# A decoder on one core: the attentions over the 77 context rows with softmax on the query side

## What is computed

```python
Q = proj_split(q, w_q)      # (B, 16, 512, 8)
K = proj_split(k, w_k)      # (B, 16, 77, 8)
V = proj_split(v, w_v)
scores = jnp.einsum('bhqd,bhkd->bhqk', Q, K) / jnp.sqrt(jnp.float32(DK))
scores = jnp.where(mask == 0, jnp.float32(-1000000000.0), scores)
attn = jax.nn.softmax(scores, axis=-1)
ctx = jnp.einsum('bhqk,bhkd->bhqd', attn, V)
ctx = ctx.transpose(0, 2, 1, 3).reshape(q.shape[0], -1, D)
return jnp.einsum('bsd,ed->bse', ctx, w_o)
```

## Time and profile before

| | us |
|---|---|
| median of 3 runs (2273.33 to 2279.63) | 2277.38 |
| the profiled execution's own time | 2252.73 |
| its span, first to last instruction | 2250.9 |
| mean granted TensorE clock in it | 0.899 |

### The profile page before, as it was taken

One profiled execution on the slowest core, in us unless ns is written; L12 is line 12 of the kernel. 1 busy time (PEld: TensorE's weight loads), 2 busy tenths in 40 slices (PEclk: granted clock), 3 DMA queues, 4 the chain that ended last, 5 costly groups with the idle time before them and its releaser, 6 DMA issues. The chain is left out here.

```text
span 2250.9 us, 34926 instructions
## 1 busy us (share of the span) xinstructions
PE 1797.8 (80%) x12404; PEld 1094.5 (49%) x12521; DVE 1477.1 (66%) x3404; ACT 1048.0 (47%) x2229; POOL 393.3 (17%) x575
## 2 busy tenths in 40 slices
PE   5768967999965999995779999993489889687872
PEld 3445542343334566663556666662245444344661
DVE  4436757888846555555546677686879999566524
ACT  2325534777721333332526555551167777365221
POOL 0110021000023444443110000001200000100374
PEclk8879977999975999998879999996589999799896
DMA  3000000000015588884000000000000000000373
GB/s 86 0 1 1 1 1 0 1 1 1 1 54 212 211 301 300 297 298 146 1 1 1 1 1 1 1 1 17 0 1 2 1 1 2 1 1 1 110 216 115
DMA packets 42797, 134.65 MB, mean 60 GB/s; under 512 B 7117, under 2 KB 22529, under 8 KB 37443
## 3 DMA queue, kind: packets, MB, share of 16 engines
q1 hardware_dynamic: 36587, 121.17, 15.5%
q0 software_dynamic: 4992, 10.23, 1.5%
q10 hardware_dynamic: 1048, 1.01, 0.2%
HBM read 123.29 MB, written 11.45 MB: 60 GB/s over the span
## 5 line engine op out<-in xcount | busy, mean ns | idle before, releaser
L153 POOL TENSOR_SCALAR rstd<-MV 128x2 f32<-128x2 f32 (+1 forms) x100 | 24.4, 244 | 1109.2 <-DVE MV L125 1102.6
L845 DVE TENSOR_REDUCE l1aM<-PS 128x2 f32<-128x1024 f32 x128 | 152.8, 1220 | 22.9 <-PE PS L601 20.8
L763 ACT ACTIVATE l1aE<-PS 128x512 f32<-128x512 f32 x256 | 140.9, 595 | 49.0 <-PE PS L630 45.6
L1575 PE MATMUL PS<-WB,H 128*128 128x512 f32 x312 | 142.6, 600 | 1.2 <-ACT H L1692 1.2
L763 ACT ACTIVATE l3aE<-PS 128x512 f32<-128x512 f32 (+3 forms) x256 | 102.5, 443 | 47.6 <-PE PS L634 44.9
L2463 DVE TENSOR_REDUCE M<-PS 128x1 f32<-128x589 f32 x128 | 92.5, 764 | 36.0 <-PE PS L2274 36.0
L845 DVE TENSOR_REDUCE l3aM<-PS 128x2 f32<-128x256 f32 (+3 forms) x128 | 101.3, 819 | 20.6 <-PE PS L603 19.6
L2372 ACT COPY PT<-PS 128x512 f32<-128x512 f32 x128 | 69.1, 590 | 92.9 <-PE PS L2285 92.6
L2378 ACT ACTIVATE E<-PS,M 128x589 f32<-128x589 f32 x128 | 95.8, 761 | 22.7 <-DVE M L2463 22.6
L1692 ACT ACTIVATE H<-PS,WB 128x128 f32<-128x128 f32 x156 | 44.5, 368 | 121.3 <-PE PS L1566 121.3
L873 DVE SCALAR_TENSOR_TENSOR l3aE<-l3aE,l3aLB 128x2048 f32<-128x2048 f32 (+1 forms) x64 | 94.9, 1483 | 2.7 <-ACT l3aE L763 2.7
(11 more groups left out here) (695 smaller groups left out, 4666.6 us busy)
## 6 DMA issues: line engine op xcount, KB each, us to landing
WB<-in_experts SPq DMA_DIRECT2D x39, 1798.0 KB
TB<-mixed_tails SPq DMA_DIRECT2D x39, 384.0 KB
WB<-in_experts SPq DMA_DIRECT2D x39, 384.0 KB, 4.2
WB<-mixed_out SPq DMA_DIRECT2D x8, 256.0 KB, 4.8
YB<-expert_out SPq DMA_DIRECT2D x8, 256.0 KB, 4.7
WB<-in_fold SPq DMA_DIRECT2D x1, 1676.0 KB, 7.0
cols_l2x_sb<-in_cols_l2x SPq DMA_DIRECT2D x1, 1154.0 KB, 10.2
mixed_tails<-in_tails SPq DMA_DIRECT2D x1, 1152.0 KB, 8.7
```

Source lines behind the costliest of these rows:

```text
L763: nc.scalar.activation(E[0:kn, home(m, kt) + j, q0:S], PS[0:kn, 4 + n % 2, q0:S], ACT.Exp, scale=SCALE).then_inc(exp_done, 1)
L845: v.tensor_reduce(M[:, m % 2, qt, 2 * hp:2 * hp + 2], PS[:, bank:bank + 2, 0:kc], AX, ALU.max, negate=True).then_inc(pair_free, 1)
L1575: mm(o, H1[:, i % 3, c * P:(c + 1) * P], mid_w(i, c), start=(c == 0), stop=False)
```

## The change

`cross_attention` takes the place of `attention16` for l0x and l3x. Q, K and V are projected once a batch (K and V for all four batches at once) and stay fp32, with the biases added. KS holds K eight times, each copy with only one head's rows of a 64-row half left (`own`), so that a product of 64 rows with four of these copies gives four heads' scores. The unit of work is S: one tile of 128 queries and eight heads, 128 x 1232 scores in two banks, made by four fp32 products, one in each 64x64 quadrant of the array, of 308 columns each (in l0x behind two bf16 mask products). There are two units to a query tile, 32 to a stage. VectorE takes the maximum over the 77 keys of each head and subtracts it into E; ScalarE takes the exponential of all 1232 in place. X turns E head by head (eight fp32 transposes into two banks, each emptied by a ScalarE copy into ET), and O multiplies, for a query tile, each of the 16 heads' turned probabilities (77 x 128, the stationary operand) with its 8 columns of V and a column of ones; VectorE divides. C, W, Y, N go by half batches, for which the norm's helpers are cut in two. `CROSS` is the order: for tile i, X of unit 2i+2, S of unit 2i+4, O of tile i, X of 2i+3, S of 2i+5, with Q, C, W, Y, N placed between by hand. GpSimd makes KS for batches 1 to 3. The three-part splits, gathers, the second scores and the turned maxima are gone in these stages. `setup` no longer loads or makes `maskT`.

```diff
+CROSS = (
+    (("X", 1, 0, 0), ("X", 1, 0, 1), ("S", 2, 0), ("O", 0), ("X", 1, 1, 0), ("X", 1, 1, 1), ("S", 2, 1)),
+    {0: ((0, ("Q", 1)), (5, ("Y", -1, 0)), (6, ("C", -1, 1))), 1: ((3, ("N", -1, 0)),),
+     2: ((0, ("W", -1, 1)), (4, ("C", 0, 0)), (5, ("Y", -1, 1))), 3: ((0, ("W", 0, 0)), (4, ("N", -1, 1)))},
+)
+def cross_attention(k, name, w, mask=None):
...
+                if kind == "K":
+                    mm(PS[:, 5, 0:BT * SC], w["wk"], k.CT[:, :, :].rearrange("p b n -> p (b n)"), start=True, stop=True).then_inc(kb_ready, 1)
...
+                elif kind == "S":
+                    n = u[1]
...
+                    if n >= 2:
+                        pe.wait_ge(shifted, n - 1)
+                    for g in range(2):
+                        if mask is not None:
+                            mm(PS[:, 2 * (n % 2) + g, 0:CW], k.ident_b, mask[:, qt:qt + 1, :].broadcast_to([P, HG, SC]), start=True, stop=False,
+                               skip_group_check=True)
+                    for half in range(2):
+                        for g in range(2):
+                            c0, rows = qt * P + 64 * half, slice(64 * g, 64 * g + 64)
+                            ins = mm(PS[64 * half:64 * half + 64, 2 * (n % 2) + g, 0:CW], Q[rows, b % 2, c0:c0 + 64],
+                                     KS[rows, b, HG * p:HG * p + HG, :].rearrange("p j n -> p (j n)"), start=mask is None, stop=True,
+                                     skip_group_check=True)
+                    ins.then_inc(s_ready, 1)
+                elif kind == "X":
+                    n, g = u[1:]
+                    if g == 0:
+                        pe.wait_ge(exped, n + 1)
+                    if n:
+                        pe.wait_ge(et_taken, 2 * n + g - 1)
...
+                    for j in range(HG):
+                        ins = nc.tensor.transpose(PS[0:SC, 4 + g, j * P:(j + 1) * P], E[:, n % 2, g, j, :], k.ident)
+                    ins.then_inc(e_turned, 1)
+                elif kind == "O":
...
+                    pe.wait_ge(et_taken, 4 * i + 4)
...
+                    for p in range(2):
+                        for g in range(2):
+                            for j in range(HG):
+                                h = HG * (p + 2 * g) + j
+                                ins = mm(PS[:, 6, h * DA:(h + 1) * DA], ET[:, (2 * i + p) % 4, HG * g + j, :], Va[:, b, h, :], start=True, stop=True)
+                    ins.then_inc(o_ready, 1)
...
+                elif kind == "S":
+                    n = u[1]
+                    act.wait_ge(shifted, n + 1)
+                    e = E[:, n % 2].rearrange("p g j n -> p (g j n)")
+                    nc.scalar.activation(e, e, ACT.Exp, scale=SCALE).then_inc(exped, 1)
+                elif kind == "X":
+                    n, g = u[1:]
+                    act.wait_ge(e_turned, 2 * n + g + 1)
...
+                    nc.scalar.copy(ET[:, n % 4, HG * g:HG * g + HG, :].rearrange("p j q -> p (j q)"), PS[0:SC, 4 + g, :]).then_inc(et_taken, 1)
...
+                elif kind == "S":
...
+                    dve.wait_ge(s_ready, n + 1)
+                    sc = PS[:, 2 * s:2 * s + 2, 0:CW].rearrange("p g (j n) -> p g j n", n=SC)
+                    v.tensor_reduce(top[:, s], sc, AX, ALU.max, negate=True).then_inc(maxed, 1)
+                    dve.wait_ge(maxed, n + 1)
+                    if n >= 2:
+                        dve.wait_ge(e_turned, 2 * n - 2)
+                    v.tensor_tensor(E[:, s], sc, top[:, s].unsqueeze(3).broadcast_to([P, 2, HG, SC]), ALU.add).then_inc(shifted, 1)
+                elif kind == "O":
+                    i = u[1]
+                    dve.wait_ge(o_ready, i + 1)
+                    o = PS[:, 6, 0:H * DA].rearrange("p (h d) -> p h d", d=DA)
+                    step(v.reciprocal(rec[:, :], o[:, :, DK]))
+                    step.wait()
...
@@
-                act.dma_start(maskT_i[:, :], dram["maskT"]).then_inc(mask_landed, 16)
@@
-                for m, o in ((mask_i, mask_b), (maskT_i, maskT_b)):
-                    step(v.tensor_scalar(o[:], m[:], 0, -1.0, ALU.not_equal, ALU.add))
-                    step.wait()
-                    step(v.tensor_scalar(o[:], o[:], -NEG, None, ALU.mult))
+                step(v.tensor_scalar(mask_b[:], mask_i[:], 0, -1.0, ALU.not_equal, ALU.add))
+                step.wait()
+                step(v.tensor_scalar(mask_b[:], mask_b[:], -NEG, None, ALU.mult))
@@
-            attention16(k, "l0x", W["l0x"], k.CT, (mask_b[:, :, :], maskT_b[:, :]))
+            cross_attention(k, "l0x", W["l0x"], mask_b[:, :, :])
@@
-            attention16(k, "l3x", W["l3x"], k.CT)
+            cross_attention(k, "l3x", W["l3x"])
```

More of the change, by code:

```diff
@@ L113, in norm_stats, with norm_half_stats, norm_half_apply @@
     def norm_stats(self, dve, y, step, b):
+        for h in HALVES:
+            self.norm_half_stats(None if y is None else y[:, h], step, b, h)
+    def norm_half_stats(self, y, step, b, h):
         v = self.nc.vector
[L116 to L119, removed]
-                step.wait()
-            for t in range(h.start, h.stop):
-                step(v.bn_stats(self.S6[:, b, t, :], self.R[:, b, t, :]))
-            step.wait()
-            for t in range(h.start, h.stop):
-                ins = v.bn_aggr(self.MV[:, b, t, :], self.S6[:, b, t, :])
-            ins.then_inc(self.statted, 1)
+        if y is not None:
+            step(v.tensor_tensor(self.R[:, b, h], y, self.X[:, b * NT + h.start:b * NT + h.stop, :], ALU.add))
+            step.wait()
+        for t in range(h.start, h.stop):
+            step(v.bn_stats(self.S6[:, b, t, :], self.R[:, b, t, :]))
+        step.wait()
+        for t in range(h.start, h.stop):
+            ins = v.bn_aggr(self.MV[:, b, t, :], self.S6[:, b, t, :])
+        ins.then_inc(self.statted, 1)
     def norm_apply(self, dve, normed, b, n):
+        for i in range(len(HALVES)):
+            self.norm_half_apply(dve, normed, b, n, i)
+    def norm_half_apply(self, dve, normed, b, n, i):
         v = self.nc.vector
[L131 to L137, removed]
+        h = HALVES[i]
+        dve.wait_ge(self.statted, 2 * n + i + 1)
+        dve.wait_ge(self.rooted, 2 * (2 * n + i) + 2)
+        for t in range(h.start, h.stop):
+            v.tensor_scalar(self.X[:, b * NT + t, :], self.R[:, b, t, :], self.MV[:, b, t, 0:1], self.rstd[:, b, t:t + 1],
+                            ALU.subtract, ALU.mult).then_inc(normed, 1)
     def norm_vector(self, dve, y, step, normed, b, n):
@@ L3044, in decoder_kernel @@
         mask_b = k.sb("mask_b", [P, NT, SC], BF16)
-        maskT_b = k.sb("maskT_b", [SC, S], BF16)
         kmask_u = k.sb("kmask_u", [1, BT, SC], U8)
@@ L3077, in setup @@
             mask_i = k.sb("mask_i", [P, NT, SC], I32)
-            maskT_i = k.sb("maskT_i", [SC, S], I32)
             causal = k.sb("causal", [P, 2, P])
@@ L3139, in _ @@
                     step(v.tensor_copy(o, const[i]))
-                dve.wait_ge(mask_landed, 48)
+                dve.wait_ge(mask_landed, 32)
                 step(v.tensor_copy(k.causal_b, causal[:, 0, :]))
                 step(v.tensor_copy(k.causalT_b, causal[:, 1, :]))
-                for m, o in ((mask_i, mask_b), (maskT_i, maskT_b)):
-                    step(v.tensor_scalar(o[:], m[:], 0, -1.0, ALU.not_equal, ALU.add))
-                    step.wait()
-                    step(v.tensor_scalar(o[:], o[:], -NEG, None, ALU.mult))
+                step(v.tensor_scalar(mask_b[:], mask_i[:], 0, -1.0, ALU.not_equal, ALU.add))
+                step.wait()
+                step(v.tensor_scalar(mask_b[:], mask_b[:], -NEG, None, ALU.mult))
                 for b in (1, 3):
@@ L3283, in packs @@
     biases.update(l0a_ball=np.concatenate([a["L0_attn_b_v"], a["L0_attn_b_shell"], a["L0_attn_b_charge"]]), l0a_bo=a["L0_attn_b_out"])
-    cols["l0x"] = attn16_pack(*(a["L0_xattn_w_" + n].T for n in "qkvo"))
+    i = np.arange(P)[:, None]
+    own8 = (i // 32 % 2 == np.arange(2 * HG) // HG) & (i // DK % HG == np.arange(2 * HG) % HG)
+    cols["l0x"] = dict(attn16_pack(*(a["L0_xattn_w_" + n].T for n in "qkvo")), own=own8)
     cols["l0f"] = dict(wr=a["L0_ffn_W_r"].T, wk=a["L0_ffn_W_k"].T, wv=a["L0_ffn_W_v"].T,
@@ L3311, in packs @@
     f = "L3_xattn_"
-    cols["l3x"] = attn16_pack(*(a[f + "W" + n] for n in "qkvo"), a[f + "bq"], a[f + "bk"])
+    cols["l3x"] = dict(attn16_pack(*(a[f + "W" + n] for n in "qkvo"), a[f + "bq"], a[f + "bk"]), own=own8)
     biases.update(l3x_bv=a[f + "bv"], l3x_bo=a[f + "bo"])
@@ L3373, in lay_out @@
               "causal": np.stack([later, later.T], 1).astype(np.float32), "decay": decay.astype(np.float32), "terms": stack_terms(),
-              "mask": mask.reshape(NT, P, SC).transpose(1, 0, 2), "maskT": mask.T,
+              "mask": mask.reshape(NT, P, SC).transpose(1, 0, 2),
               "kmask": kmask.reshape(B, 1, SC), "experts3": experts3.reshape(8 * P, 6 * P)}
```

159 lines of the change are left out of this document (added).

## The result

The changed kernel takes 2330.4 us (median of 4 runs, 2308.3 to 2334.8) beside 2276.3 us for the kernel before (4 runs, 2273.3 to 2279.6): a ratio of 1.0218, 95% interval 1.015 to 1.0286. The forecast was 2332.0.

The account below looks back on a forecast made before the run. No engine bounds the whole kernel, but both stages are mostly bound by TensorE. Terms of 5.4 + 8.3 + 26 + 13 + 2 give 54.7 us slower: 2307.5 us profiled, 2332 as a median; range 2282 to 2365.

Parts of the forecast that it names:

- The bound: Both stages, l0x and l3x: mostly bound by TensorE, busy 123 of 145 and 112 of 142 us before the change.
- VectorE and ScalarE: Per tile in both stages, priced for 1232 scores a unit: VectorE 7.2 us, ScalarE 4.8 and 0.5 us.
- TensorE at 2.4 GHz: TensorE's work a tile at full clock: 7.7 us in l3x, 8.3 in l0x, of which O 3.5 us.
- The hand-over and the score unit: VectorE and TensorE waiting for each other make tiles 8.2 us (l3x) and 8.55 (l0x); a score unit takes 0.95 us.
- the walk: Tile order followed, 15.5 tiles plus head and tail: l3x 147.3 us (+5.4), l0x 152.8 us (+8.3).
- The clock: Falls to 1.2 GHz behind O, 1.75 us each: one a tile in l3x (26 us), one in two in l0x (13).
- The sum: Both stages together: 5.4 + 8.3 + 26 + 13 + 2 = 54.7 us slower, 2332 us as a median.
- carried-over 24.6 us: Whole kernel: the earlier runs' median, 2277.38 us, lay 24.6 above the profiled execution; this difference was added unchanged.
- The clock holds: Rival, chance 0.20: X and S may carry the clock over O in both stages; +14 us, 2291 us.
- VectorE-bound: Rival, chance 0.08: O's pairs overlap at 0.05 us each, VectorE sets tiles of 7.4 us; 19 us saved, 2258 us.
- Low clock throughout: Rival, chance 0.05: the clock stays low in both stages, tiles of 14.3 and 15.3 us; 2501 us.
- Quadrants one after the other: Rival, chance 0.03: score products run serially, 2.9 us a tile more; 2380 us if the clock is held.

Follow-up runs that it names:

- spread order: The changed kernel with O cut in four parts between the tile's transposes and scores; 2241.8 us beside 2250.5 for the kernel before, ratio 0.9949.
- 117-column kernel: The changed kernel with O's products 117 columns wide instead of 9, heads ascending; 2267.4 us beside 2275.9 for the kernel before, ratio 0.996.
- strips: The changed kernel with O's operands exchanged: V loaded, probabilities stream, four heads in four column strips; 2220.7 us beside 2275.9 for the kernel before, ratio 0.9753.

## Why the prediction was right, and where it was right by luck

*The bound.* Right: TensorE busy 161.6 of 167.3 us in l3x, VectorE waiting 83 us for it.

*VectorE and ScalarE.* Wrong by a factor: 616 elements a unit are 0.80 us for the maximum, 0.80 for the subtraction and 0.72 for the exponential, so VectorE needs 4 x 0.80 + 0.5 + 0.9 = 4.6 us a tile and not 7.2 (73.4/16 = 4.6), ScalarE 4.1 and not 5.3. The 616-element row (0.795 us) stood in rows 4; I scaled it to a size that two banks of 512 can't even hold. Counting the heads of a unit against its columns would have caught it.

*TensorE at 2.4 GHz.* O was right (3.6 us, said 3.5), and so were the transposes (0.9 to 1.0 for eight). A score unit was priced too high: 0.68 us, said 0.95, from a round of 16 instructions of another shape. That is 0.54 a tile, nearly all by which the spread order's 7.1 us lies under my sum of 7.7 for l3x; in l0x it is 7.5 against 8.3.

*The hand-over and the score unit.* These are the first two terms that failed. I added 0.5 and 0.25 us a tile for two engines close to each other. No such wait is there once the clock holds. Windows of l3x between head and tail, of the spread kernel and of the 117-column kernel, whose order of units is the one that I walked through:

```profile
1945.00:2052.00 107.00, 106.74 (x982) 89.40 (x974) 62.69 (x122) 53.83 (x103) 4.62 (x10) 0.99 0.01 1
1945.00:2052.00 107.00, 105.00 (x931) 84.50 (x923) 61.36 (x120) 53.81 (x98) 4.74 (x11) 0.98 0.01 1
```

TensorE is busy for 106.7 and 105.0 of 107 us. Over 15.5 tiles and two stages the hand-over was 12 us of the walk, the score unit's 0.54 us a tile 17, together the 29 us by which the walk was too long. That VectorE's 4.6 us instead of 7.2 is why the hand-over fell away is argued: VectorE's work was doubled only in the changed kernel, where the clock falls, and in strips. With the clock held, l3x takes 136.4 us and not 147.3, l0x 142.6 and not 152.8: against rows 3 that is 5.5 and 1.9 us **faster** than before, where I had 5.4 and 8.3 slower. 21.1 us too much in all; the 117-column kernel (142.7 and 136.8 us) says the same, 20.6. The row of maxima shows where: from the first maximum to the last subtraction it is 112 us in l3x and 118.5 in l0x, where I had 127 and 132.5; head and tail together were 4 us longer in each stage than I had them, part of it because they run at the low clock.

*The clock.* The mechanism was right: the clock falls in or just behind O, and O's loads are 0.11 us apart at 1.00 and 0.21 at 0.50. Every experiment that gave TensorE more columns beside O's loads, whatever they were (63, 117, transposes, or the tile's own work in between), raised the mean clock and shortened the stages. Its size is the other term that failed, most of it in l0x. The same work in another order is 30.9 us shorter in l3x (167.3 - 136.4) and 28.1 in l0x (170.7 - 142.6; 19.8 by the other length of l0x). I had 27 and 14. By the record of the granted clock it comes out the same: l3x has 82.0 us at the low level in the changed kernel and 20.3 in the spread one, l0x 71.7 and 16.3; half of the differences is 30.9 and 27.7. The falls in l3x, 14, were nearly as many as I took (15). In l0x the mask products didn't halve them (12, not 7.5). And a fall could cost more than I had priced. Of the 25 low stretches that go with an O, 12 began behind it, and each lasted 3.4 us, about what I had priced. The other 13 began inside an O, which I hadn't thought of: 12 of them lasted twice that or more, with the rest of O at the low level too. Whether that rest is why they lasted longer isn't shown.

*The sum.* 21.1 us too much for the hand-over and the score unit, less the longer heads and tails, and 18.0 too little for the clock (59.0 against 41, my two microseconds for the tails counted with the latter). They cancel to 3: 51.6 measured for both stages, 54.7 said. The time was right to 2 us, with two large terms each wrong by about 20; that they cancelled was luck, and the changed kernel's own runs spread over more than those 2 us, from 2308 to 2337. The carried-over 24.6 us fits the last stretch, 24.5 us longer in one profile than in the other, and could be carried. Setup and GpSimd's product (1.83 us the first, 4.2 for three) cost nothing that can be seen.

*The rivals.* "The clock holds" was priced at 14 us slower. The spread and the 117-column kernels are that case, and they are 9 and 8 us faster than before. Its chance would have had to go to "faster". "VectorE-bound" was a rival without ground: VectorE needs 4.6 us, so O at half its price would have left TensorE the bound at 7.1 - 1.8 = 5.3 us. In strips, where most of O's price is gone, VectorE was still busy for only 72 of 116 us of l3x. "Low clock throughout" was right in this much, that in l3x the clock was low half of the time. "Quadrants one after the other" is out: 0.68 us a unit.

## What to carry to other kernels

When one engine is full and its clock is granted by activity, ask of each long row of instructions how much it streams beside its loads: O was 3.6 us of loads with 9 columns each, and standing in one piece it cost 59 us in two stages. The cure is first an order that puts dense work between the parts. Then the operands can be exchanged, so that the wide one streams and the narrow one is loaded, with several of the narrow ones side by side in the array. And check a price for the number of elements by the memory that has to hold them; a forecast that comes out right can rest on two errors, which only runs that move one term alone can show.

## What the hardware showed that I had not expected

Work added made the stages shorter: 16 transposes a tile more took 14.8 us off l3x, and 13 times the columns took 30.5 us off it (136.8 beside 167.3). A pair of fp32 load (128 columns) and product starts every 0.11 us whether it streams 9 or 117 columns. Doubling VectorE's work in the strips kernel lowered TensorE's mean clock from 0.97 to 0.88, with nothing changed on TensorE. In the changed kernel a fall behind O lasted 3.4 us each time, and one inside O 6.8 us or more in 12 of 13 cases. And one untouched stage took 169 us on one occasion and 191 to 194 on others, in every kernel; what makes the difference stays open.
